# Both up products of the MLP side by side, on two pairs of PSUM banks, in steps without transforms

## The reference: what is computed

```
def _block(x, ...):
    residual = x
    xn = _ln(transpose(x), ln1w, ln1b)            # LayerNorm over the 64 channels
    xf = rfft2(xn)                                # 128 x 128 transform of every channel
    o1 = relu(complex xf @ w1 + b1)
    o2 = o1 @ w2 + b2, masked where |re| and |im| are both under 0.01
    x = residual + irfft2(o2)
    xp2 = _ln(transpose(x), ln2w, ln2b)
    h = gelu(xp2 @ mw1 + mb1)                     # 64 -> 256
    m = h @ mw2 + mb2                             # 256 -> 64
    return x + m
```

## Time and profile before

| | before |
|---|---|
| median of 3 runs | 3672.34 us (3670.01 to 3673.15) |
| the profiled execution | 3670.97 us |
| its span, first to last instruction | 3669.2 us |
| TensorE busy | 3269.5 us, 89% |
| DVE, ScalarE, GpSimd busy | 2379.5, 2338.8, 1640.9 us |
| mean granted TensorE clock | 0.957 |
| first and last up product of the AFNO stage | 459.4 and 3234.3 us |

### The profile page before, as it was taken

One profiled execution on the slowest core, in us unless ns is written; L12 is line 12 of the kernel. 1 busy time (PEld: TensorE's weight loads), 2 busy tenths in 40 slices (PEclk: granted clock), 3 DMA queues, 4 the chain that ended last, 5 costly groups with the idle time before them and its releaser, 6 DMA issues. The chain is left out here.

```text
span 3669.2 us, 53038 instructions
## 1 busy us (share of the span) xinstructions
PE 3269.5 (89%) x18280; PEld 1974.7 (54%) x18280; DVE 2379.5 (65%) x4145; ACT 2338.8 (64%) x3752; POOL 1640.9 (45%) x1365
## 2 busy tenths in 40 slices
PE   4953699999999999998989999999999999979579
PEld 1742555656565646464646464646464646344247
DVE  3935676767676666676766676766666664536477
ACT  1944576767676767676767676767666666646358
POOL 4405554555545554545454545455454543210142
PEclk8976899999999999999999999999999999989789
DMA  8871111111111111313121101010111111168788
GB/s 283 261 231 46 46 64 41 52 47 47 52 41 52 47 47 46 113 49 126 59 75 41 64 30 64 30 64 32 67 41 52 41 52 41 64 229 234 242 280 241
DMA packets 267993, 342.60 MB, mean 93 GB/s; under 512 B 36928, under 2 KB 210752, under 8 KB 259552
## 3 DMA queue, kind: packets, MB, share of 16 engines
q1 hardware_dynamic: 246832, 323.66, 25.8%
q0 software_dynamic: 6960, 14.05, 1.4%
q10 hardware_dynamic: 13952, 1.68, 0.4%
HBM read 192.38 MB, written 146.93 MB: 92 GB/s over the span
## 5 line engine op out<-in xcount | busy, mean ns | idle before, releaser
L1511 ACT ACTIVATE a_hidden<-a_wide,a_up_b 128x1024 f32<-128x1024 f32 x512 | 568.7, 1111 | 138.1 <-PE a_wide L1690 136.6
L1690 PE MATMUL a_wide<-a_yc,a_up_fold 64*128 64x512 f32 x2048 | 583.8, 646 | 44.2 <-ACT a_hidden L1511 40.0
L1701 PE MATMUL a_result<-a_hidden,a_down 128*64 128x512 f32 x2048 | 509.0, 618 | 38.0 <-ACT a_hidden L1511 33.7
L1259 POOL TENSOR_TENSOR a_y<-a_o,a_mag 128x256 f32<-128x256 f32 (+1 forms) x512 | 365.0, 738 | 386.6 <-DVE a_mag L1354 386.6
L1217 POOL TENSOR_TENSOR a_y<-a_x,a_stat 128x512 f32<-128x512 f32 x256 | 267.4, 1045 | 556.4 <-DVEq L1399 539.7
L1337 DVE TENSOR_TENSOR a_o<-a_bank,a_mix_b 128x512 f32<-128x512 f32 (+1 forms) x272 | 181.4, 667 | 275.2 <-PE a_bank L1647 269.5
L1665 PEld LDWEIGHTS a_bank<-a_dft_h,a_g 128*128 128x128 f32 x2080 | 272.9, 192 | 129.5 <-issue 129.5
L1647 PEld LDWEIGHTS a_bank<-a_mix,a_o 128*128 128x128 f32 x2080 | 252.9, 191 | 149.9 <-issue 132.1
L1524 ACT ACTIVATE a_delta<-a_result,a_down_b 128x512 f32<-128x512 f32 x256 | 175.8, 687 | 237.3 <-PE a_result L1701 237.3
L1384 DVE TENSOR_REDUCE a_stat<-a_sq 128x16 f32<-128x1024 f32 x240 | 290.5, 1211 | 32.1 <-ACT a_sq L1545 30.7
L1365 DVE TENSOR_TENSOR a_x<-a_result,a_x 128x512 f32<-128x512 f32 x256 | 175.8, 687 | 203.0 <-PE a_result L1716 202.4
(11 more groups left out here) (191 smaller groups left out, 6181.7 us busy)
## 6 DMA issues: line engine op xcount, KB each, us to landing
a_x<-rows SPq DMA_DIRECT2D x112, 512.0 KB, 4.4
rows<-a_x SPq DMA_DIRECT2D x112, 512.0 KB, 2.6
box_xc<-in_x SPq DMA_DIRECT2D x16, 1024.0 KB, 13.2
box_x<-in_x SPq DMA_DIRECT2D x64, 256.0 KB, 4.3
turned<-box_o SPq DMA_DIRECT2D x64, 256.0 KB, 3.5
a_y<-turned SPq DMA_DIRECT2D x16, 1024.0 KB, 10.4
box_x<-rows SPq DMA_DIRECT2D x16, 1024.0 KB, 24.3
planes<-box_work SPq DMA_DIRECT2D x64, 256.0 KB, 3.4
```

Of the source, the lines that this page charges most:

```text
L1259: ins = G.tensor_tensor(y[n % 2][:, :, to].rearrange("p c k -> p k c"), o2[:, j % 3, lo:4, r], mask[:, lo:4], ALU.mult)
L1511: A(hidden[:, i % 2, j], wide[:], ACT.Gelu, bias=up_b2[:, l, j:j + 1]).then_inc(s_hid, 1)
L1690: mm = M(wide[:, half * BANK:(half + 1) * BANK], up_fold[cs, l, j * P:(j + 1) * P], yc[cs, i % 2], start=True, stop=True)
L1701: mm = M(result[half * C:(half + 1) * C, :], down[:, l, j, :], hidden[:, i % 2, j, half * BANK:(half + 1) * BANK], start=j == 0, stop=j == ...
```

## The change

Steps without transforms are called light: q in 2, 3, 14, 15, and q from 5 in the last run. Banks 2 and 3 become one tensor `pair` of two adjacent banks; the transforms use the same two banks through slices of it. In a light step, up 1 writes into `pair` instead of `wide`, and TensorE issues it directly behind up 0, ahead of turn_back and turn. What up 1 waits for is new: the gelu 1 of the step before, if that step was light too (it read `pair`); else the last DVE add of the inverse part that used the pair: part 3 of the next run in step 14, part 5 in step 2, part 7 in step 5 of the last run. Up 0 behind a light step waits for one gelu less. All other steps, and the orders of ScalarE, DVE, GpSimd and the DMA queue, stay as they are.

```diff
         turned, result = psum("turned"), psum("result")
-        bank = [psum(f"bank{i}") for i in range(4)]
+        pair = psum("pair", 2 * BANK)
+        bank = [psum("bank0")[:], psum("bank1")[:], pair[:, 0:BANK], pair[:, BANK:2 * BANK]]
...
+        def light(i):
+
+            n, q = divmod(i, BLOCKS)
+            return q in (2, 3, 14, 15) or n == RUNS - 1 and q >= 5
+
+        def hidden_area(i, j):
+            return pair if j and light(i) else wide
...
-                    A(hidden[:, i % 2, j], wide[:], ACT.Gelu, bias=up_b2[:, l, j:j + 1]).then_inc(s_hid, 1)
+                    A(hidden[:, i % 2, j], hidden_area(i, j)[:], ACT.Gelu, bias=up_b2[:, l, j:j + 1]).then_inc(s_hid, 1)
...
                 def mlp_up(i, j):
                     l = layer_of(i // BLOCKS)
                     pe.wait_ge(s_yc, i + 1)
-                    if i or j:
-                        pe.wait_ge(s_hid, HC * i + j)
+                    n, q = divmod(i, BLOCKS)
+                    if j and light(i):
+                        if light(i - 1):
+                            pe.wait_ge(s_hid, HC * i)
+                        elif q == 14:
+                            pe.wait_ge(s_x, INVERSES * (n + 1) + 4)
+                        else:
+                            pe.wait_ge(s_x, INVERSES * n + (6 if q == 2 else 8))
+                    elif i or j:
+                        pe.wait_ge(s_hid, HC * i + j - (j == 0 and light(i - 1)))
                     for half in range(2):
                         cs = slice(half * C, (half + 1) * C)
-                        mm = M(wide[:, half * BANK:(half + 1) * BANK], up_fold[cs, l, j * P:(j + 1) * P], yc[cs, i % 2],
+                        mm = M(hidden_area(i, j)[:, half * BANK:(half + 1) * BANK], up_fold[cs, l, j * P:(j + 1) * P], yc[cs, i % 2],
                                start=True, stop=True)
                     mm.then_inc(s_up, 1)
...
                     if mlp:
                         mlp_up(Q, 0)
+                    if mlp and light(Q):
+                        mlp_up(Q, 1)
                     parts(n, q, 0, inverse, forward, spectrum, backward)
...
                     parts(n, q, 1, inverse, forward, spectrum, backward)
-                    if mlp:
+                    if mlp and not light(Q):
                         mlp_up(Q, 1)
```

## The result

| | before | after |
|---|---|---|
| median of 5 runs | 3672.34 us | 3707.78 us (3705.58 to 3713.29) |
| ratio to before | | 1.0102, interval 1.0091 to 1.0113 (33 to 41 us) |
| the profiled execution | 3670.97 us | 3705.58 us |
| its span | 3669.2 us | 3703.8 us |
| TensorE busy | 3269.5 us | 3281.1 us |

What follows compares the result with a forecast made beforehand. TensorE, busy 3269.5 of 3669.2 us, was taken as the bound. Waits (a to e) +30.8 and clock +17.8 gave +48.6 on 3670.97 = 3719.6; with the median 1.4 higher, 3721 us, range 3700 to 3739.

Steps and rivals of the forecast that it cites:

- the main term: Step 2 of each run: up 1 waits for the inverse transform's last DVE add; 30.6 us over 16 runs.
- rival 1: The clock holds in the new idles, so only the waits cost: 3703 us; chance 0.22.
- The falls at step 0: Longer idle before step 0's turn drops the clock in five runs: 5 x 1.27 = 6.4 us.
- c: Steps 3: +0.15 us in each of 14, less about 0.5 in runs 6 and 7; together +1.1 us.
- e: Run 15: step 5 waits for the transform's add, +0.8 us; ten further steps lose 0.15; together +2.3 us.
- d: Steps 14, 15 and next step 0: DVE and GpSimd set the time; gains only after some runs, together -3.2 us.
- b: Step 2: up 1 waits until the pair is free; +1.99 us in 14 runs, +1.35 in two, sum 30.6.
- the falls in step 2: Step 2's new idle drops the granted clock in nine of 14 runs: 9 x 1.27 = 11.4 us.
- Step a: Light steps: without up 1 as cover, the 1.53 us residual chain shows; 5.52 us against 5.37, +0.15 each.
- Step f: Granted clock falls behind new idles at step 2 (11.4 us) and at step 0 (6.4 us): +17.8 us.

Runs made afterwards that it cites:

- experiment 2: Kernel before the change, with only step 2 of each run changed, all other steps as before: 3711.83 us, ratio 1.0109.
- experiment 3: Changed kernel with the pair on banks 0 and 1 instead of 2 and 3, same order: 3670.68 us, ratio 1.0000.
- experiment 5: Changed kernel, pair still on banks 2 and 3, but up 1 at its old place behind turn_back and turn: 3666.34 us, ratio 0.9988.
- experiment 1: Changed kernel, but step 2 keeps its old order and old banks: 3670.50 us, ratio 0.9999.
- experiment 6: Changed kernel with two extra matmuls, output unread, ahead of up 1's wait in step 2: 3702.10 us, ratio 1.0081.
- experiment 7: Changed kernel with the pair on banks 0 and 1 and up 1 between turn_back and turn: 3669.89 us, ratio 0.9998.
- run 15: Not a follow-up: the last of the 16 runs of steps inside the kernel's AFNO stage; its end measured +0.3 us in the changed kernel.
- experiment 4: Changed kernel with the pair on banks 0 and 1 and up 1 at its old place behind both transposes: 3657.79 us, ratio 0.9963.
- experiment 8: Kernel before the change, with only step 2 changed and its wait filled with two extra matmuls, output unread: 3703.68 us, ratio 1.0089.

## Why the prediction came out as it did

The sign, the place and the size of the main term were right, and the measured time lies inside the range. It lies 13 us under the forecast, nearer to rival 1 (3703) by the number, but not by its mechanism: the clock did fall in step 2, in 11 steps. Of the 13 us, 8.1 lie in the stage (48.6 forecast, 40.5 measured). The falls at step 0, which did not come, are 6.4 of them. The terms c and e were forecast 4.2 too high and d 0.3; against that, b was forecast 0.9 too low and the falls in step 2 1.9 too low.

*Step b, the pair must be free:* right in runs 1 to 14. The step lost 2.00 us in each of the three runs 1, 4 and 14, whose clock held; 1.99 were forecast. Down was released by DVE and up 1 by L1320 in all of them. Run 0 lost 2.13 where 1.35 was forecast: before, the clock had fallen in its step 1, and in the changed kernel it did not, so that step was 1.65 us shorter and DVE's add came later in step 2. In experiment 2, where it fell there as before, run 0 lost 1.37. Experiments 2 and 3 show that the loss comes from the pair's last reader. The prediction counted the order's share in it without separating it; experiment 5 does: three quarters come from what is queued behind the wait.

*Step a, the residual chain:* the chain is right to the hundredth (1387.84 to 1389.37 is 1.53), but its effect was mis-sized, and with it steps c and e. I took 1.06 us for each product. Side by side they take 0.96 each (1385.92 to 1387.84 is 1.92). So the step takes 5.32 us, not 5.52; the loss of 0.15 is a gain of 0.05. That is 0.2 us in 24 steps, 4.8 us. In runs 6 and 7, steps 3 and 4 together won 0.4 us and not 1.0, since the steps 4 lost most of what the steps 3 won.

*Step d:* right. Steps 14 to 0 are bound by DVE and GpSimd, and what the waits gave back was 3.5 us for 3.2 forecast.

*Step f, the clock:* the first half was right and a little small (13.3 for 11.4). The second half was wrong for this kernel, and is the larger miss, 6.4 us. I reasoned from the five runs in which the clock had held at step 14 before. In the changed kernel it held in none: it fell in 14 of 14 steps 14, where nothing is lost by it, and so the idle of step 0 stayed short, 0.86 us in run 6 (step 15 of run 5 and the turn of the next step 0):

```profile
1541.06 1.94 PE L1718 MATMUL a_result<-a_hidden,a_down 128*64 128x512 f32 x8 [0.44 <-DVE a_x L1374]
...
1545.50 0.66 PE L1727 MATMUL a_turned<-a_ident,a_y 128*128 128x128 f32 x4 [0.86 <-POOL a_y L1226]
```

Where falls at step 14 are fewer (9 or 10 of 14: experiments 1, 3, 6, 7), each step 14 that holds is followed by a fall in step 0, at about 1.6 us net. So the mechanism and its condition were sound; what failed is the count, that the clock would hold at five steps 14 as it had before. Why it fell at all 14 is not shown.

The other 5 of the 13 us lie outside the stage, in the spread of code that the change doesn't touch. The rule on many small idles that cycle through banks (the Trainium skill, TensorE: Matmul & The Clock Gate, "A second HAM failure mode: psum-queue depth-cycling") is not borne out by the idles of 0.44 us in run 15's steps, behind which the clock stayed at 1.00. "HAM oscillation" on the same page of the Trainium skill reports of one kernel that doubled PSUM buffers brought nothing more. That does not carry over to experiment 4, where they brought 13 us.

## What to carry to other kernels

A second buffer borrowed from another stage is free only once that stage's last reader is done, so look in that reader's queue first: here two other banks of the same size, whose reader runs one step earlier, turned +35 us into 0. And a product that waits for one thing may be the cover for another: take the wait away and leave the product where it stands (13 us gained, 9 of them traced), and don't put a new wait at the head of an in-order queue, ahead of work that is ready. Time that is gained where another engine sets the pace comes back as idle, and the clock may charge for it.

## What the hardware showed unexpectedly

- Two up products directly behind one another take 1.92 us; one between groups of another kind, or behind a wait, takes 1.06. The wait cost more than it lasted: 0.28 us of idle, taken away, shortened the step by 0.35.
- Equal idles do not bring equal falls. The clock fell in step 2 of 11 of runs 1 to 14, behind idles of 1.9 and 2.1 us, and held in the other three, whose idle was 2.1 us too. In the changed kernel and in experiment 2 it fell at step 14 of all 14 runs, one after the other; before it fell at nine of them, and in experiments 6 and 8, whose step 2 is filled, at nine and ten. What decides it is not shown.
- Idle moved is not idle saved. Keeping the clock up in step 2 (experiment 6) brought six falls at step 0, and with steps 14 and 15 shortened every step 14 whose clock held (18 of 18) was followed by a fall at the next step 0.
